# Moving layer 0's weighted expert sum for five batches from VectorE to ScalarE and GpSimd

## The reference

```python
x = x + jnp.tanh(g_xattn[0]) * _L0_xattn_ref(_layernorm(x), ctx, ctx, mask, ...)
x = x + jnp.tanh(g_ffn[0]) * _L0_ffn_ref(_layernorm(x), ...)     # 8 experts, top 2
x = x + jnp.tanh(g_xattn[1]) * _L1_xattn_ref(_layernorm(x), ctx, ctx, ...)
x = x + jnp.tanh(g_ffn[1]) * _L1_ffn_ref(_layernorm(x), ...)     # 8 experts, top 2
```

## Time and profile before

| | us |
|---|---|
| median of 3 runs | 771.39 |
| lowest, highest | 769.09, 775.52 |
| the profiled execution's own time | 765.87 |
| its span (first to last instruction) | 764.1 |
| PE busy in the span | 670.0 (88%) |
| DVE busy | 427.7 (56%) |
| ACT busy | 274.1 (36%) |
| POOL busy | 213.9 (28%) |

### The profile page before, as it was taken

The page is one execution under the profiler, slowest core; times in us unless marked ns, Lnnn a source line. Parts: engine busy times, 40 slices in busy tenths (PEclk is TensorE's granted clock), DMA queues, the critical chain, the costliest instruction groups (busy, mean ns, idle before and its releaser), DMA issues. The chain is left out here.

```text
span 764.1 us, 17540 instructions
## 1 busy us (share of the span) xinstructions
PE 670.0 (88%) x5804; PEld 514.1 (67%) x5804; DVE 427.7 (56%) x1481; ACT 274.1 (36%) x528; POOL 213.9 (28%) x399
## 2 busy tenths in 40 slices
PE   5798999759999999999999999978888885999970
PEld 3576777537777777777777777656666664788860
DVE  4777999853333433233233233469999996454426
ACT  3566566511211211111212112245655542354540
POOL 4122554470111111111111111112245546344440
PEclk9999999959999999999999999999999996899995
DMA  9033564561132131101101110330121232544429
GB/s 222 15 124 132 185 199 147 153 217 38 55 98 61 36 80 36 35 28 35 35 28 35 36 28 22 108 128 30 30 79 64 71 99 77 150 129 121 123 84 329
DMA packets 50857, 70.71 MB, mean 93 GB/s; under 512 B 7688, under 2 KB 38024, under 8 KB 50772
## 3 DMA queue, kind: packets, MB, share of 16 engines
q1 hardware_dynamic: 42380, 50.85, 22.3%
q0 software_dynamic: 6816, 18.69, 6.9%
q10 hardware_dynamic: 1575, 0.05, 0.2%
HBM read 46.55 MB, written 23.02 MB: 91 GB/s over the span
## 5 line engine op out<-in xcount | busy, mean ns | idle before, releaser
L1488 PE MATMUL ps<-w_all,share 128*128 x780 | 232.3, 445 | 3.7 <-DVE share L1124 3.7
L1488 PEld LDWEIGHTS ps<-w_all,share 128*128 128x128 f32 x780 | 146.8, 193 | 66.2 <-issue 8.4
L551 POOL DMA_INDIRECT ys_dram<-share,dest_i x78 | 75.5, 968 | 332.6 <-DVE share L1135 280.0
L1518 PE MATMUL ps<-w_all,share 112*128 (+1 forms) x624 | 148.0, 380 | 1.8 <-ACT share L737 1.0
L1518 PEld LDWEIGHTS ps<-w_all,share 112*128 112x128 f32 (+1 forms) x624 | 112.4, 190 | 15.1 <-issue 2.6
L1151 DVE TENSOR_TENSOR share<-share,ps 128x344 f32<-128x344 f32 x78 | 40.1, 514 | 141.0 <-PE ps L1488 79.8
L726 ACT COPY share<-ps 128x512 f32<-128x512 f32 x39 | 22.9, 586 | 151.9 <-PE ps L1501 151.9
L840 DVE TENSOR_REDUCE m_f<-ps 128x8 f32<-128x960 f32 x64 | 70.3, 1138 | 10.9 <-PE ps L1260 10.8
L723 ACT ACTIVATE share<-ps 128x344 f32<-128x344 f32 x78 | 35.7, 458 | 107.2 <-PE ps L1488 107.2
L544 POOL DMA_INDIRECT xs_dram<-xn,slot_now x64 | 64.0, 1000 | 21.9 <-issue 14.6
L514 POOL TENSOR_SCALAR nm<-mv 128x1 f32<-128x1 f32 (+1 forms) x48 | 12.2, 253 | 160.9 <-DVE mv L887 112.2
(11 more groups left out here) (204 smaller groups left out, 996.5 us busy)
## 6 DMA issues: line engine op xcount, KB each, us to landing
share<-xs_dram SPq DMA_DIRECT2D x78, 129.0 KB, 2.2
w_all<-ys_dram SPq DMA_DIRECT2D x16, 512.0 KB, 6.9
w_all<-gate SPq DMA_DIRECT2D x8, 688.0 KB
w_all<-up SPq DMA_DIRECT2D x8, 688.0 KB
w_all<-down SPq DMA_DIRECT2D x8, 560.0 KB
w_all<-w SPq DMA_DIRECT2D x16, 256.0 KB
xs_dram<-q_flat SPq DMA_DIRECT2D x17, 129.0 KB, 2.3
out<-x_sb SPq DMA_DIRECT2D x8, 256.0 KB, 5.2
```

What stands on the lines that cost most here:

```text
L551: g.indirect_dma_start(ys_dram, bass.IndirectOffsetOnAxis(ap=dest_i[:, u:u + 1], axis=0), y_sb[:, u, :], None).then_inc(D_y[u], 16)
L1488: i = t.matmul(ps[:, bank, 0:w], xgT[:, k, :], w_all[:, bass.ds(off + (k * UPW[l] + col - EW[l]), w)], start=(k == 0), stop=(k == KT - 1))
L1518: i = t.matmul(ps[:, 6, 0:D], hT[0:r, c + KD[1] * (j % 2) * l, :], w_all[0:r, bass.ds(off + (KT * UPW[l] + c * D - EW[l]), D)], start=(c = ...
```

## The change

Batches 3 to 7 of layer 0's results (`BY_V = 3`) are no longer combined by VectorE in layer 1's attention. In their place:

- ScalarE multiplies the gathered results in place, `weigh(b, k)`: two ACTIVATEs (Copy with a scale per partition) of 128x256 for each choice k. Both choices of batch 3 in unit 0; then choice 1 of batch b+3 at the end of an even unit and choice 0 of batch b+4 at the end of an odd one (choice 0 of a batch therefore comes one unit ahead of choice 1).
- GpSimd adds them to the tokens, `add_results(b, k)`: one TENSOR_TENSOR of 128x512 for each choice, both at the end of odd units 1, 3, 5, 7 and 9, for batches 3 to 7. The second waits for the first.
- VectorE waits for GpSimd's semaphore `g_sum` where it had the combine, ahead of `ln1_stats`.
- Batches 0, 1 and 2 and the final combine stay with VectorE; the counts that wait for it are changed.

```diff
+        BY_V = 3
@@ SP
-                sp.wait_ge(d_comb, NT + 2 * (b + 1))
+                sp.wait_ge(d_comb, 2 * BY_V + 2 * (b + 1))
@@ GpSimd
+            def add_results(b, k):
+
+                g.wait_ge(a_wy, 2 * (b - BY_V) + k + 1)
+                if k:
+                    g.wait_ge(g_sum, 2 * (b - BY_V) + 1)
+                g.tensor_tensor(x_sb[:, 2 * b:2 * b + 2, :], x_sb[:, 2 * b:2 * b + 2, :], yg[:, b, :, k, :],
+                                ALU.add).then_inc(g_sum, 1)
@@
                     if u > 0:
                         ln2_rstd(G - 1)
+                    if l == 1 and not even and BY_V <= b + 3 < NB:
+                        add_results(b + 3, 0)
+                        add_results(b + 3, 1)
@@ ScalarE
+                def weigh(b, k):
+
+                    a.wait_ge(D_gl[b], 16)
+                    a.wait_ge(C_v, 8)
+                    for t in range(2):
+                        i = a.activation(yg[:, b, t, k, :], yg[:, b, t, k, :], ACT.Copy, scale=wcomb[:, 2 * b + t, k:k + 1])
+                    i.then_inc(a_wy, 1)
@@
                     if u >= 1:
                         ln2_apply(G - 1)
+                    if l == 1 and u == 0:
+                        weigh(BY_V, 0)
+                    if l == 1 and even and b + 3 < NB:
+                        weigh(b + 3, 1)
+                    if l == 1 and not even and b + 4 < NB:
+                        weigh(b + 4, 0)
@@ VectorE
-                                v.wait_ge(d_c1, 2 * (NB * L + b) + t + 1)
+                                v.wait_ge(d_c1, 2 * (BY_V * L + b) + t + 1)
@@
                         if l == 1:
-                            combine(0, b + 2)
-                            v.wait_ge(d_comb, 2 * (b + 2) + 2)
+                            if b + 2 < BY_V:
+                                combine(0, b + 2)
+                                v.wait_ge(d_comb, 2 * (b + 2) + 2)
+                            else:
+                                v.wait_ge(g_sum, 2 * (b + 3 - BY_V))
                         ln1_stats(B + 2)
```

More of the change, by code:

```diff
@@ L278, in flamingo_kernel @@
         d_comb, d_c1 = (sem(n) for n in ("combined", "combine_step"))
+        a_wy, g_sum = (sem(n) for n in ("results_weighted", "results_added"))
         g_ve2, g_pw2, g_rs2, g_ve1, g_pw1, g_rs1 = (sem(n) for n in (
```

## The result

The changed kernel's median is 771.55 us beside 769.93 us for the kernel before, 20 executions each. The ratio is 1.0032, interval 1.0017 to 1.0046: 2.5 us slower (1.3 to 3.5), within the 1% that stands for no change. The forecast was 2.7 us faster.

The account below looks back on a forecast made before the run. VectorE was taken to bound layer 1's attention (busy 106.17 of 115 us). 7.5 us won minus 4.85 held gives 2.7 faster, 771.4 to 768.7 us, range 763.5 to 775.5.

Parts of the forecast that it names:

- Removed work: VectorE, layer 1's attention: five combines gone, 0.84 us won in unit 2 and 1.67 in units 4, 6, 8, 10; ceiling 7.5.
- ScalarE: Twenty added ACTIVATEs, 1.09 us per pair, 10.9 in all, covered by waits; no table reload; unit 0 at worst 0.5.
- Price of an add: GpSimd, each TENSOR_TENSOR of 128x512: 1.24 us taken, between a lower end of 0.62 and an upper of 2.04.
- The hold: Odd units 1 to 9: VectorE's divisions held behind one GpSimd add, 0.97 us each, 4.85 us in all.
- GpSimd's longer chain: Units with a scatter: chain of 16.7 us until `divide`, free beside held divisions; otherwise 0.9 in every other pair, 1.8 in all.
- The pair of 16.1 us: Profile after, attention stage: a pair of units takes 16.1 us, not 16.8.
- The sum: Whole kernel: 7.5 us won minus 4.85 held gives 2.7 us faster, 768.7 us.
- Rival D: Stage shorter, but the clock, half speed around 635 to 656 us, takes back or adds a microsecond or two; no separate chance.
- A: GpSimd's adds and VectorE's divisions don't hold each other up; GpSimd's chain bounds: 5.7 us won, 765.7; chance 0.22.
- B: Full ceiling of 7.5 us won, 763.9: adds at 0.62 and divisions not held; pairs 15.1 us; chance 0.08.
- C: VectorE's divisions held behind both adds, 2.2 us per odd unit: 3.5 us slower, 774.9; decides from 1.5 per unit; chance 0.2.
- the forecast's own band: Whole kernel's time between 766.5 and 771 us, likeliest 768.7; chance 0.45.

Follow-up runs that it names:

- adds behind the divisions: Changed kernel plus one wait, so GpSimd's adds start behind VectorE's divisions of the same unit: 770.82 us, ratio 1.0006 to the kernel before.
- the run with the gap filled: Changed kernel plus six idle TensorE matmuls of 128x32 behind the shifted scores in even units 2 to 10: 768.38 us, ratio 0.9980 to the kernel before.
- adds off the divisions: Changed kernel with the adds ahead of `ln2_rstd`, waiting for the previous unit's divisions: 763.90 us, ratio 0.9931 to before; 0.9842, 0.9831, 0.9822 on the second chip kind.
- with and without the work: Second chip kind, ratios to before: changed kernel with adds ahead of `ln2_rstd`, 0.9822; changed kernel without weighting and adds, 0.9818 (0.9801 in an earlier set).
- hold alone: Kernel before, all combines kept, plus two idle GpSimd adds in odd units 1 to 9, second chip kind: 797.08 and 797.56 us, ratios 0.9878 and 0.9891.

## Why the prediction was wrong

**Removed work: right.** The ceiling of 7.5 us, as 0.84 and 4 x 1.67, is measured: 7.38 in the stage, 0.82 (15.09 to 14.27) in the first pair and 1.63 to 1.65 in each of the next four. What VectorE no longer executes does shorten the stage one for one.

**ScalarE: right.** 0.90 us a pair for 1.09 estimated, no table reload, nothing on the path; in unit 0, where 0.5 was feared, nothing either (7.76 us between the `row_max` of units 0 and 1, 7.77 before).

**Price of an add: right enough.** 1.31 us on the mean (1.27 alone, up to 1.42 beside VectorE) for 1.24 taken, inside the bounds of 0.62 and 2.04. The Trainium skill's 4497 ns for 2048 elements (GPSIMD Engine Reference, 3.1 Elementwise) scale in plain proportion to an estimate of 1.12, a little below the 1.2 that the prediction wrote; 1.27 was measured.

**The hold: right.** One add, as forecast: 4.75 us over five units for 4.85. Of the rows that it was read from the earlier trace rows, the CAST at 488.25 was nearer to the case than the L868 at 518.49, whose neighbour moved two elements. (The CAST also had one of GpSimd's scatter instructions beside it, from 487.76 to 488.72, so it was behind more than the MEMSET.) The Trainium skill's rule (SBUF — State Buffer, Who interferes with whom) says that a VectorE instruction with two SBUF inputs and a GpSimd one that reads SBUF exclude each other. For adds of 128x512 the trace agrees: every division that was held ended within 0.15 us of the add's end. For the tiny ones it doesn't: the divisions that overlap GpSimd's TENSOR_TENSOR of 128x2 keep their 0.49, though the rule makes no exception for them; the measurement decides. The trace adds a detail: in units 5, 7 and 9 the first of the two divisions is the one held (1155 ns in place of 292). In units 1 and 3 it is the second division (1359 ns).

**GpSimd's longer chain: right for this kernel, too cheap without the hold.** (Its terms add up to 16.6, not 16.7, which changes nothing.) In the changed kernel it costs nothing beside the hold (`ln1_apply` waits 0.5 in all). Without the hold, and with the adds at the end of the chain, it does bind (adds behind the divisions), at 1.76 in the pair without a slow stretch and in three pairs in a row, not 0.9 in every other; those adds also start later, though.

**The pair of 16.1 us: right where the clock stays.** 15.98 in the two undisturbed pairs of the run with the gap filled, 16.03 to 16.05 by the account.

**The sum: this failed.** "7.5 won - 4.85 held = 2.7 us" has no term for what the hold does to TensorE. The prediction followed the held division only along VectorE, to `cT`, `out_proj` and the next `row_max`. It didn't ask what TensorE does meanwhile. TensorE's gap ahead of the routing logits was 0.86 and became 1.73, by the length of the hold, and its clock was known to fall elsewhere in this very trace. Rival D had the right mechanism and the wrong place: it let the clock change only behind the stage ("the half-speed stretch around 635 to 656"). The missing term is 3.96 us: three stretches of 3.4 us at half speed at 1.3 each. 7.38 - 4.75 - 3.96 = -1.33, the measured 1.32 longer stage. That a stretch costs this much is shown apart from the sum: 15.98 for 17.36 in the run with the gap filled, 15.34 for 16.91 in two runs of the changed kernel.

**The rivals.** A (no hold) and B fell as to what this change does; the version with the adds elsewhere, which has no hold, shows B's pairs (15.1 forecast, 15.16 measured) and not A's 15.6. C had the right sign for a wrong reason: VectorE is held behind one add, not two, and the 1.5 us per odd unit from which it decides is reached all the same, as hold plus clock: (4.75 + 3.96) / 5 = 1.74.

**Chances and range.** 771.55 lies within 763.5 to 775.5 and within 1%. That is no credit to the working: the range covers gain and loss alike, the forecast's own band (766.5 to 771) missed, and beside 20 executions of the kernel before (769.93, where the prediction had 771.39 from three) the sign is the wrong one.

**Left open.** The stage accounts for 1.3 of the 2.5 us; the rest lies within what executions of one kernel differ by, and isn't located. The number of slow stretches differs between executions as well (two and five in the two runs of this kernel on the second kind of chip), so the 3.96 us belong to one execution and are not the mean. Of the version with the adds off the divisions, the profiled execution is 7.7 below that of before (758.20 to 765.87), the median only 5.7 below; its other executions had a lower granted clock (0.948 to 0.956, where the profiled one had 0.967), from which stage I can't tell. The later runs on the second kind of chip (0.9822, with and without the work alike) don't settle it. And what exactly makes the clock fall behind one gap and not another is open too.

## What to carry to other kernels

When a stall is priced, follow it to every engine that waits for the stalled one, and ask above all whether TensorE's idle time grows: in three of five units a hold of 0.9 us on VectorE cost another 1.3 us through the clock. Work that is moved to GpSimd should be placed beside VectorE instructions that read PSUM or that don't matter, ahead of the chain that others wait for and not at its end; here that choice of place alone made 0.3% slower into 0.7% faster on one kind of chip. And where one chip shows waits that another does not, compare the undisturbed stretches before the totals.

## What the hardware showed beyond expectation

- Behind gaps of 1.2 to 2.0 us in TensorE came stretches of 3.4 us at a granted clock of 0.5, though not behind every such gap, and although TensorE was busy 15.03 of 17.34 us in such a pair. Each cost 1.3 to 1.6 us in the kernels with the combines taken off VectorE and the divisions held, and 0.0 to 0.7 in the kernel with the idle adds.
- A VectorE division of 128x128 from SBUF that met a GpSimd add of 128x512 took 1.16 to 1.36 us in place of 0.29. The same adds beside a reduction out of PSUM cost the reduction nothing (2.18 us in both).
- On the second kind of chip the exp stood still for 3.4 us and the residual for 1.9 with no releaser on the core; in the changed kernel and in hold alone such stops came only after 620 us, in the kernel before from 574 us on.
